# Attended products of linear attention in three equal passes, and seven reorderings at the seams of a four-stage kernel

## The reference

```
x = x + silu(xn @ W[e].T) * (xn @ W[e].T) @ W[e]     # L0 "attention": one of 4 experts by token id,
                                                     # here with ctx slices as the weights
x = x + bitlinear(value * silu(gate))                # L0 FFN, activations to 8 bits by row maximum, weights ternary
q, k = phi(xn Wq), phi(ctx Wk);  v = ctx Wv          # L1 linear attention, 16 heads of 32
attn = (q @ (k^T v)) / (q @ sum(k) + 1e-6)
x = x + (attn * sigmoid(xn Wg + bg)) @ Wo
x = x + shared_ffn(xn) + sum over 4 of 16 experts of expert_ffn(xn)   # L1 FFN, top-4 routing, capacity 256
```

## Time and profile before

| | |
|---|---|
| median of 3 executions | 1035.55 us (1035.06 to 1035.56) |
| the profiled execution | 1035.02 us |
| its span, first to last instruction | 1033.3 us |
| PE busy | 1016.5 us (98%), 5697 matmuls |
| PEld busy | 802.7 us (78%), 5720 loads |
| DVE busy | 694.8 us (67%) |
| ACT busy | 599.7 us (58%) |
| POOL busy | 282.9 us (27%) |
| mean granted TensorE clock | 0.998 of full |

### The profile page before, as it was taken

One profiled execution on the slowest core, in us unless ns is written; L12 is line 12 of the kernel. 1 busy time (PEld: TensorE's weight loads), 2 busy tenths in 40 slices (PEclk: granted clock), 3 DMA queues, 4 the chain that ended last, 5 costly groups with the idle time before them and its releaser, 6 DMA issues. The chain is left out here.

```text
span 1033.3 us, 16225 instructions
## 1 busy us (share of the span) xinstructions
PE 1016.5 (98%) x5697; PEld 802.7 (78%) x5720; DVE 694.8 (67%) x1364; ACT 599.7 (58%) x953; POOL 282.9 (27%) x444
## 2 busy tenths in 40 slices
PE   9999999999999999999999999999999999999996
PEld 6888888876455555578888888888888999999995
DVE  7758555448999998678777775677724666666661
ACT  6776788746889998863433344111203466666662
POOL 1022222124655553110000034100010154555542
PEclk9999999999999999999999999999999999999999
DMA  6693666522010000301121332302053588888863
GB/s 235 239 331 114 184 187 200 154 72 84 21 28 25 22 21 1 102 13 62 62 62 51 105 129 85 117 11 81 2 194 107 207 231 228 231 245 248 236 155 45
DMA packets 50339, 127.29 MB, mean 123 GB/s; under 512 B 5856, under 2 KB 9952, under 8 KB 49504
## 3 DMA queue, kind: packets, MB, share of 16 engines
q1 hardware_dynamic: 39248, 97.79, 28.2%
q0 software_dynamic: 10448, 27.58, 11.4%
q10 hardware_dynamic: 576, 1.05, 0.3%
HBM read 98.02 MB, written 28.38 MB: 122 GB/s over the span
## 5 line engine op out<-in xcount | busy, mean ns | idle before, releaser
L1455 PE MATMUL bank<-w,f_qT 128*128 128x512 bf16 x496 | 116.3, 379 | 1.6 <-DVE f_h L1745 0.6
L2196 POOL DMA_INDIRECT out<-e_y,scatter_idx x32 | 69.0, 2157 | 110.5 <-ACT e_y L2291 96.7
L1455 PEld LDWEIGHTS bank<-w,f_qT 128*128 128x128 bf16 x512 | 48.4, 98 | 51.7 <-DVE f_h L1745 1.6
L2234 ACT ACTIVATE s_m_h<-s_mid 128x512 fp32r<-128x512 f32 (+1 forms) x24 | 15.2, 632 | 108.3 <-DVE s_mid L2549 60.6
L2182 POOL DMA_INDIRECT e_xg<-xn_rows,gather_idx x32 | 32.4, 1012 | 166.1 <-DVE gather_idx L2539 99.2
L2646 DVE TENSOR_TENSOR e_mid<-bank,e_sil 128x256 f32<-128x256 f32 (+1 forms) x48 | 20.2, 420 | 61.4 <-ACT e_sil L2265 52.8
L1476 PE MATMUL bank<-w,f_q2T 128*128 128x512 bf16 x249 | 57.3, 379 | 0.7 <-ACT f_q2T L1182 0.3
L1745 DVE SCALAR_TENSOR_TENSOR f_h<-bank,f_columns,f_sg 128x512 f32<-128x512 f32 x64 | 47.9, 749 | 11.5 <-PE bank L1455 6.0
L54 PE MATMUL bank<-e_xT_h,e_wg_h 128*128 128x256 f32 (+1 forms) x192 | 55.3, 288 | 0.0
L54 PE MATMUL bank<-wkv_h,ctx_h_all 128*128 128x512 f32 x128 | 51.7, 404 | 2.9 <-PEq L95 1.4
L56 PE MATMUL bank<-e_xT_h,e_wg_l 128*128 128x256 f32 (+1 forms) x192 | 54.1, 282 | 0.0
(11 more groups left out here) (451 smaller groups left out, 3294.9 us busy)
## 6 DMA issues: line engine op xcount, KB each, us to landing
wraw<-in_wffn SPq DMA_DIRECT2D x48, 512.0 KB, 4.3
e_raw_g<-in_ew_gate SPq DMA_DIRECT2D x16, 704.0 KB
e_raw_u<-in_ew_up SPq DMA_DIRECT2D x16, 704.0 KB
e_raw_d<-in_ew_down SPq DMA_DIRECT2D x16, 512.0 KB
sorted_y<-e_y SPq DMA_DIRECT2D x19, 256.0 KB
x_rows<-rows SPq DMA_DIRECT2D x16, 256.0 KB, 2.0
xn_rows<-a_work SPq DMA_DIRECT2D x16, 256.0 KB, 2.0
s_raw<-x_rows SPq DMA_DIRECT2D x16, 256.0 KB, 2.6
```

The lines of the kernel that those rows point to most:

```text
L1455: ins = pe.matmul(bank[c % 2][:, :], qT[t % 2][:, k * P:(k + 1) * P], w_gv(k, col + c * 512), start=(k == 0), stop=(k == KD - 1))
L2196: gp.indirect_dma_start(io["out"], bass.IndirectOffsetOnAxis(g.scatter_idx[:, slot:slot + 1], 0), e_y[t][u][:, :], None, compute_op=ALU.ad ...
```

## The change

The diff has six edits.

1. *First tile.* `project_first` replaces `project(0)`: for each half, first the four high-times-high passes, each waiting only for the high part of its weights, then the eight passes that need a low part.
2. *Quantised layer's head.* At i = 0 `reach(0)` is split: the maximum over the first 1024 columns before `product(1,0)`, over the other 1024 after it, and a maximum of the two.
3. *Attended products.* All four chunks are made by `mm3` with 132 columns; the summary lies in two tiles, high and low; `copy_low` and its semaphores go; `a_weigh` reads both chunks of a bank by one instruction each for the denominators and the numerators.
4. *s = 1.* `gate(2)` comes before `project(0)`.
5. *End of attention.* The gate half of the shared `expand(0, 0)` comes before `turn_att(15)`, the up half after it.
6. *Last expert.* Tile t = 1 is made in two halves of 256 columns in two banks; the halves of chunk 0 come before t = 0's chunk 2, whose low part is late. ACT copies the first half, DVE the second, and POOL's last scatter waits for both.

```diff
+                def project_first():
+                    ch, cl = g.ctx_h, g.ctx_l
+                    pe.wait_ge(s["c0_hi"], 1)
+                    for half, bank, hi, lo, ready in ((0, kbank, "wk_hi", "wk_lo", "k_ready"), (1, vbank, "wv_hi", "wv_lo", "v_ready")):
+                        mine = slice(half * D, (half + 1) * D)
+                        for k in range(KD):
+                            pe.wait_ge(s[hi], k + 1)
+                            pe.matmul(bank[0][:, :], ch[:, 0, k * P:(k + 1) * P], wkv_h[:, k, mine], start=(k == 0), stop=False)
+                        for k in range(KD):
+                            if k == 0:
+                                pe.wait_ge(s["c0_lo"], 1)
+                            pe.wait_ge(s[lo], k + 1)
+                            pe.matmul(... ch ..., wkv_l[:, k, mine], start=False, stop=False)
+                            last = pe.matmul(... cl ..., wkv_h[:, k, mine], start=False, stop=(k == KD - 1))
+                        last.then_inc(s[ready], 1)
...
                     for c in range(KD):
-                        high, low = [x[:, c * S + t * P:c * S + (t + 1) * P] for x in a_q[b % 2]]
-                        bank = nbank[c // 2]
-                        if c % 2 == 0:
-                            pe.matmul(bank[:, 0:2 * SW], high, summ[:, c, :, :].rearrange("p a n -> p (a n)"), start=True, stop=False)
-                            pe.matmul(bank[:, 0:SW], low, summ[:, c, 0, :], start=False, stop=False)
-                        else:
-                            last = mm3(pe, bank[:, 2 * SW:3 * SW], (high, low), [summ[:, c, part, :] for part in range(2)], False, True)
+                        last = mm3(pe, nbank[c // 2][:, (c % 2) * SW:(c % 2 + 1) * SW], [x[:, c * S + t * P:c * S + (t + 1) * P] for x in a_q[b % 2]],
+                                   [x[:, c * SW:(c + 1) * SW] for x in summ], c % 2 == 0, c % 2 == 1)
...
-                        if s != 1:
+                        if s == 1:
+                            gate(2)
+                            project(0)
+                        else:
                             query(s + KD + 1)
-                        if s:
-                            project(s - 1)
-                        gate(s + 1)
+                            if s:
+                                project(s - 1)
+                            gate(s + 1)
...
-                turn_att(TT - 1)
                 pe.wait_ge(nz_ready, 2 * TT)
                 pe.wait_ge(th_ready, TT)
                 pe.wait_ge(feature_ready, CT + TT)
-                shared["expand"](0, 0)
+                shared["expand"](0, 0, (0,))
+                turn_att(TT - 1)
+                shared["expand"](0, 0, (1,))
                 project(TT - 1)
...
+                def reach_half(n):
+                    v.wait_ge(h2_ready, 2 * n + 2)
+                    v.tensor_reduce(am2[1 - n][:, :], h2[0][:, half(n)], AX.X, ALU.max, apply_absolute_value=True).then_inc(am2_ready, 1)
+                    if n == 1:
+                        v.wait_ge(am2_ready, 2)
+                        v.tensor_tensor(am2[0][:, :], am2[0][:, :], am2[1][:, :], ALU.max).then_inc(am2_ready, 1)
...
                     if i == 0:
+                        reach_half(0)
                         product(1, 0)
-                    reach(i)
+                        reach_half(1)
+                    else:
+                        reach(i)
...
 (a_weigh, new)
+                    for half in range(2):
+                        ins = v.tensor_scalar(dz[...], both[half][:, :, P:SW], ATT_EPS, 2.0, ALU.add, ALU.mult)
+                    ...
+                    v.reciprocal(z[:, :], dz[:, :]).then_inc(z_ready, 1)
+                    ...
+                    for half in range(2):
+                        v.tensor_tensor(mine[2 chunks], both[half][:, :, 0:P], z[2 chunks, broadcast], ALU.mult).then_inc(nz_ready, 1)
...
+        def contract_last():
+            i, u = PAIRS - 1, 1
+            ...
+            pe.wait_ge(e_m_lo, seq(i, u, 0))
+            part(0, 0, e_obank[u][0][:, :], whole)
+            pe.wait_ge(e_m_lo, seq(i, u, 1))
+            part(0, 1, e_obank[u][0][:, :], whole)
+            pe.wait_ge(e_y_ready[0], 2 * PAIRS)
+            halves(0)
+            pe.wait_ge(e_m_lo, seq(i, u, 2))
+            part(0, 2, e_obank[u][0][:, :], whole).then_inc(e_o_ready[u], 1)
+            halves(1)
+            halves(2)
...
 (POOL, add)
+                if e == E1 - 1 and t == 1:
+                    gp.wait_ge(e_y_ready[0], 2 * PAIRS + 1)
```

More of the change, by code:

```diff
@@ L881, in ffn0_to_experts1 @@
         raw_q = low.take("a1_raw_q", [P, KD * D], fp32)
-        summ = after_wq.take("a1_summ", [P, KD, 2, SW], f32r)
+        summ = [after_wq.take(f"a1_summ_{n}", [P, KD * SW], f32r) for n in "hl"]
         aT = [after_wq.take(f"a1_aT_{n}", [P, KD, P], f32r) for n in "hl"]
@@ L1803, in a_weigh @@
                 def a_weigh(s):
+                    v.wait_ge(n_ready, s + 1)
+                    both = [x[:, 0:2 * SW].rearrange("p (k n) -> p k n", n=SW) for x in nbank]
+                    for half in range(2):
+                        ins = v.tensor_scalar(dz[:, half * 2 * NH:(half + 1) * 2 * NH].rearrange("p (k h) -> p k h", h=NH), both[half][:, :, P:SW],
+                                              ATT_EPS, 2.0, ALU.add, ALU.mult)
+                    ins.then_inc(dz_ready, 1)
+                    v.wait_ge(dz_ready, s + 1)
+                    v.reciprocal(z[:, :], dz[:, :]).then_inc(z_ready, 1)
+                    v.wait_ge(z_ready, s + 1)
                     if s >= 2:
@@ L2290, in turn @@
                         act.wait_ge(e_o_ready[u], i * 2 + (t + 1))
+                        if t == 1 and not exists(after):
+                            act.activation(e_y[1][1][:, 0:HALF], last_banks[0][:, 0:HALF], ACT.Copy, scale=g.slot_weight[:, SLOTS - 1:SLOTS]).then_inc(e_y_ready[1], 1)
+                            continue
                         act.activation(e_y[t][u][:, :], e_obank[u][t][:, :], ACT.Copy, scale=g.slot_weight[:, bass.ds(i * 4 + (2 * u + t), 1)]).then_inc(e_y_ready[u], 1)
@@ L2297, in tensor, with expand @@
     def tensor(pe):
-        def expand(b, c):
+        def expand(b, c, halves=(0, 1)):
             n = b * SFT + c
@@ L2309, in expand @@
                 return
-            for w, bank, ready in ((wg, gbank, g_ready), (wu, ubank, u_ready)):
+            for half in halves:
+                w, bank, ready = ((wg, gbank, g_ready), (wu, ubank, u_ready))[half]
                 for k in range(KD):
@@ L2379, in e_expand, with part, halves @@
             last.then_inc(gu_ready, 1)
+        def contract_last():
+            i, u = PAIRS - 1, 1
+            def part(t, c, bank, cols):
+                r = ROWS[c]
+                return mm3(pe, bank, [x[0:r, c, t * P:(t + 1) * P] for x in e_m[u]], [x[0:r, c, cols] for x in e_wd[u]], c == 0, c == FT - 1)
+            def halves(c):
+                for n in range(2):
+                    cols = slice(n * HALF, (n + 1) * HALF)
+                    last = part(1, c, last_banks[n][:, 0:HALF], cols)
+                    if c == FT - 1:
+                        last.then_inc(e_o_ready[1 - n], 1)
+            whole = slice(0, D)
+            pe.wait_ge(e_m_lo, seq(i, u, 0))
[8 more added lines that the diff above has]
+            halves(2)
         def body():
@@ L2405, in turn @@
                         pe.wait_ge(e_y_ready[u], i * 2)
+                    if not exists(after):
+                        contract_last()
+                        continue
                     for t in range(2):
```

53 lines of the change are left out of this document (17 added, 36 removed).

## The result

| | before | changed |
|---|---|---|
| median of the timed runs, us | 1035.64 (1035.06 to 1037.37) | 1037.24 (1036.53 to 3036.04) |
| span of the profiled execution, us | 1033.3 | 1035.3 |
| start of the last scatter on POOL, us | 1026.29 | 1027.98 |

The ratio of the times is 1.0016, 95% interval 1.001 to 1.0022: 1.6 us slower, inside the forecast's own range. (The title counts seven reorderings; the diff has five edits beside the attended products.) The longest run of the changed kernel is a single one far from all others and is left out of the comparison.

A forecast was written before the change was run, and what follows sets the result against it. PE, busy 98% of the span, bounds the kernel. Terms +3.2 + 0.5 - 0.43 - 0.73 - 0.19 - 0.35 - 0.17 = +1.85 us on the median 1035.55 gave 1037.4 us, range 1036.7 to 1038.2.

The forecast's parts named there:

- What bounds the kernel: Whole kernel: PE, busy 98%, sets the time; less ACT or DVE work gains nothing by itself, only visible PE waits count.
- Edit 3's passes: Attended products: twelve passes instead of ten, each costing its weight load of 0.112 us, over 16 tiles +3.2 us.
- Rival A: Attended products: narrow passes cost their columns, a shared stationary is free, so no loss there; 1034.2 us; chance 6%.
- Edit 1: First tile: the late fourth high part moves the value half from 10.01 to 10.52; +0.5 us, which stays.
- rival D: First tile: PE's clock falls to half, the following some 16 passes cost 3.0 to 3.7 us more; 1040.7 us; chance 5%.
- Rival B: First tile: fourth piece lands in time, costing 0.2 or gaining up to 0.3 us; 1036.6 to 1037.1 us; chance 10%.
- Edit 2: Quantised head: the split reduction uses DVE's idle 0.69 us, so `product(1,1)` comes earlier; -0.43 us.
- Edits 4 and 5: Wide passes cover PE's stops: -0.73 us at s = 1, -0.19 one tile later, -0.35 at the end of attention.
- what is late next: nothing: After s = 1: no later chain makes PE wait, each being covered by 2.8 us of passes.
- Edit 6: Last expert: PE's idle is filled, but POOL's scatter pace limits the gain to -0.17 us.
- C: Head and end of attention: a new wait eats gains, 0.8 us or 0.5 more; 1038.2 or 1038.7 us; chance 24%.
- The sum: Whole kernel: all terms together make +1.85 us, giving 1037.4 us, slower but just inside the 0.2% measuring limit.

The follow-up runs named there:

- experiment 1: Kernel before with only the twelve narrow attended passes, the new `a_weigh` and no ACT copies: 1037.69 us, ratio 1.0021.
- experiment 4: Changed kernel without the high-queries times low-summary pass of the two odd chunks, ten narrow passes a group (result incomplete): 1033.8 us, one run.
- experiment 5: Changed kernel with the first tile's old pass order: 1036.53 us, ratio 1.0009.
- 3: Changed kernel with old attended products, per-k-step pass order in the first tile, and both last-expert row groups in halves: 1034.61 us, ratio 0.9992.
- 7: Kernel before with only the first tile reordered, per k-step high x high, low x high, high x low: 1035.31 us, ratio 0.9998.
- experiment 2: Changed kernel with the attended products, `a_weigh` and copies of before: 1034.68 us, ratio 0.9991.

## Why the prediction was right, step by step

- **What bounds the kernel**: right. 12.4 us off DVE and 8.3 off ACT bought 0.98 us (experiment 1), and only through three visible stops.
- **Edit 3's passes**: 3.15 measured, 3.2 forecast. The even spacing of the loads in the earlier trace rows was the right row to go by. The second argument for it was wrong: 5720 loads against 5697 matmuls is not passes that reload, but 23 matmul records that the trace lacks (every pass has one load in the other traces). Rival A is out: experiment 4 prices a pass on an unchanged stationary at 0.112 us. The 81 ns of the Trainium skill ("TensorE: Matmul & The Clock Gate", section "Back-to-back issue gap") are not met here, at a granted clock of 1.00 in the attention window.
- **Edit 1**: the mechanism and the place were right (fourth high part in fourth place), +0.61 against +0.5 at the first tile. The fourth pass starts at 8.40 as forecast (8.37), and in the four traces with the four high passes ahead the value half begins 2.25 to 2.27 us behind the end of the fourth high part, wherever that lies (8.35 to 8.67). But the restart after the stop adds 0.1 us: its follower comes 0.34 behind it, not 0.24. "All the front is PE's own pace, so the loss stays" was too simple: it grows to 0.83 at the head, where PE waits for DVE and DVE for ACT (experiment 5). PE began at 6.79, not at the 6.3 of rival D: its dummy matmuls stood ahead, and the 14 of them took 5.87 us here against 4.74 in the kernel before, since they ran for longer at 0.43 us each, twice the 0.22 of such a pass later on (the lower of the clock's two levels, 1.2 GHz). It cost nothing, for the fourth pass had to wait anyhow. PE's row in both kernels, before and changed:

```profile
1.27 4.74 PE L586 MATMUL bank<-idle_rows 128*128 128x512 bf16 x14 [1.27 <-DVE idle_rows L755]
...
1.27 5.87 PE L603 MATMUL bank<-idle_rows 128*128 128x512 bf16 x14 [1.27 <-DVE idle_rows L772]
```

- **Rival B** did not come: in those four traces the value half began at 10.62, 10.89, 10.92 and 10.74. ACT went on to the fourth piece without waiting in three of the eleven profiled executions (experiments 1, 3 and 7), but none of these had this order.
- **Edit 2**: the first half of the reduction takes 1.12 to its follower, the second 1.25; my estimate was 1.24 for both. So `product(1,1)` gains 0.53 on DVE instead of 0.43, and PE a further 0.2 behind it. In the changed kernel 0.22 of this is spent on what edit 1 adds, which leaves the 0.52 of the table.
- **Edits 4 and 5**: sizes right (-0.74, -0.21, -0.43), credit wrong. The forecast said that of edit 3 "only the visible waits can answer; they are counted in edits 4 and 5". Experiment 1 shows edit 3 alone earning 0.38 + 0.17 + 0.43 = 0.98 of those 1.38 us. The sum holds since a stop can be removed only once; but what it gave edit 4 (0.92, of which it put 0.19 down to the shorter `a_weigh`) and edit 5 (0.35) is not theirs alone. Beside edit 3, edit 4 is worth some 0.4 and edit 5 nothing; without edit 3, edit 4 wins 0.71 at s = 1 and loses 0.34 at the next tile (experiment 2), so that "what is late next: nothing" holds for the changed kernel alone, thanks to the shorter `a_weigh`.
- **Edit 6**: -0.17, as forecast, set by POOL's two scatters 1.86 us apart where it had been 2.03. Edits 2, 5 and 6 never ran alone; their sizes come from the traces.
- **Rivals C and D**: in the changed kernel no new wait and no fall of the clock (0.998 over the execution) came up; passes were 0.23 us apart behind 8.7 us. A new wait of the kind that C feared does come without edit 3, at `project(1)` (experiment 2). D's price, some 16 passes at half the clock, stands in no row of these traces and stays untested.
- **The sum**: +1.85 forecast (its terms add up to 1.83), +1.69 at the last scatter, +2.0 in the span (the tail behind the last scatter was 7.3 us instead of 7.0), +1.6 timed. That it met so well is in part luck: the loss of edit 1 was 0.3 us larger than forecast, and the gain of edit 2 as much. A measurement tells more than the 0.2% that the forecast allowed it: the interval of the ratio leaves out 1.

## What to carry to other kernels

With PE at 98%, count weight loads: in this kernel fp32 passes of up to 264 columns with 128x128 loads cost the load, so two products of one stationary belong side by side in one pass wherever the bank has room, and splitting them costs a full slot (0.112 us) even if it frees other engines of tens of instructions. Several edits aimed at one stop share one gain, so price them together, and run each alone before giving it credit. When a stop behind a split or a copy is left, look at what stands ahead of it in its engine's queue: one step moved past a wait of 0.67 us was worth more than a reordering of PE.

## What the runs showed of the hardware that I had not expected

- The first context tile's transfer landed at another time in each profiled execution: ACT began on it between 5.03 and 5.64 us, with the same instructions ahead of it. In the old order of the first tile PE's start moves with it (7.14 at 5.04, 7.45 at 5.35).
- A pass of 264 columns costs 0.01 us more than one of 132: ten loads took 1.14 us with two wide passes, 1.12 with none (experiment 4).
- After a stop the first pass of 512 columns takes 0.47 to 0.51 us instead of 0.40 and its follower comes up to 0.1 us later (8.40 to 8.74 here, 464.58 to 464.92 in experiment 1; 7.14 to 7.45 in the kernel before), so a stop of 0.3 us costs up to 0.4. A change from narrow to wide passes without a stop costs 0.05 of this (464.31 to 464.60 in the changed kernel).
